# TensorE's period in a decoder's self-attention: the two pairs for the maxima moved behind the fourth score and the small product

## What is computed

```python
q, k, v = proj(Wq, bq), proj(Wk, bk), proj(Wv, bv)        # 16 heads of 16
attn = einsum('bhld,bhrd->bhlr', q, k) * scale            # 1024 x 1024 per head
dist = clip(arange(L)[None, :] - arange(L)[:, None], -64, 8) + 64
rel  = einsum('bhld,lrd->bhlr', q, dist_emb[dist]) * scale
out  = einsum('bhlr,bhrd->bhld', softmax(attn + rel), v)  # then @ Wo.T + bo
```

## Time and profile before

| | |
|---|---|
| median of 3 runs | 1447.9 us (1444.5 to 1449.9) |
| the profiled execution | 1447.09 us, its span 1445.3 us |
| mean granted TensorE clock | 0.953 |
| PE / PEld busy | 1286.4 / 683.0 us |
| DVE / ACT / POOL busy | 1043.6 / 949.5 / 335.6 us |
| DMA | 273.13 MB, 189 GB/s on average |

### The profile page before, as it was taken

One profiled execution on the slowest core, in us unless ns is written; L12 is line 12 of the kernel. 1 busy time (PEld: TensorE's weight loads), 2 busy tenths in 40 slices (PEclk: granted clock), 3 DMA queues, 4 the chain that ended last, 5 costly groups with the idle time before them and its releaser, 6 DMA issues. The chain is left out here.

```text
span 1445.3 us, 24911 instructions
## 1 busy us (share of the span) xinstructions
PE 1286.4 (89%) x8220; PEld 683.0 (47%) x8220; DVE 1043.6 (72%) x2547; ACT 949.5 (66%) x1666; POOL 335.6 (23%) x567
## 2 busy tenths in 40 slices
PE   7787999999999999999999999999997799910597
PEld 4444344344334334334434434436886587710586
DVE  3376778887887887887887887872564457999655
ACT  4434777777777777777777777773775558959600
POOL 4544121211211211212112112004452002320012
PEclk9999999999999999999999999999998899965799
DMA  8999977877878788697697796526321313825032
GB/s 237 308 335 265 241 206 232 222 202 236 224 215 219 217 234 213 200 260 208 193 259 211 197 249 190 188 74 181 103 74 44 131 59 116 314 87 211 4 113 88
DMA packets 263758, 273.13 MB, mean 189 GB/s; under 512 B 66222, under 2 KB 246990, under 8 KB 259534
## 3 DMA queue, kind: packets, MB, share of 16 engines
q1 hardware_dynamic: 261998, 268.39, 63.9%
q10 hardware_dynamic: 1632, 3.15, 0.7%
HBM read 153.69 MB, written 117.00 MB: 187 GB/s over the span
## 5 line engine op out<-in xcount | busy, mean ns | idle before, releaser
L603 ACT ACTIVATE pr<-scoresT 128x512 f32<-128x512 f32 x1024 | 550.5, 600 | 224.2 <-PE scoresT L851 162.9
L847 PE MATMUL scoresT<-qT,kT 99*128 99x512 bf16 (+7 forms) x1408 | 359.2, 326 | 5.5 <-DVE attn_out L740 2.3
L695 DVE CUSTOM_DVE_ANT_0 junk<-scores_for_max,win 128x200 f32<-128x200 f32 (+2 forms) x512 | 180.1, 352 | 172.4 <-PE scores_for_max L822 162.3
L700 DVE TENSOR_REDUCE mx<-scores_for_max 128x1 f32<-128x888 f32 (+6 forms) x448 | 301.6, 673 | 0.0
L698 DVE TENSOR_REDUCE mx<-scores_for_max 128x1 f32<-128x64 f32 (+6 forms) x448 | 277.4, 619 | 0.0
L864 PE MATMUL attn_out<-pr,vS 128*17 128x512 f32 x2048 | 271.1, 601 | 6.0 <-DMA vS<-v_all 5.9
L847 PEld LDWEIGHTS scoresT<-qT,kT 99*128 99x128 bf16 (+1 forms) x1408 | 113.6, 97 | 335.6 <-ACT rows L580 97.8
L851 PE MATMUL scoresT<-idf,win 128*128 128x128 f32 x1024 | 218.2, 274 | 0.0
L477 POOL COPY rows<-rows 128x736 f32<-128x736 f32 x128 | 102.2, 798 | 391.4 <-ACT rows L580 391.4
L821 PE MATMUL scores_for_max<-kX,qT 64*128 64x512 bf16 x512 | 164.8, 384 | 4.3 <-DVE mx L700 3.0
L822 PE MATMUL scores_for_max<-kX,qX 64*128 64x512 bf16 x512 | 164.7, 384 | 0.0
(11 more groups left out here) (203 smaller groups left out, 1757.3 us busy)
## 6 DMA issues: line engine op xcount, KB each, us to landing
rel_table<-rows SPq DMA_DIRECT2D x128, 512.0 KB, 4.8
win<-rel_table SPq DMA_DIRECT2D x128, 512.0 KB, 5.4
up_raw<-xT_normed SPq DMA_DIRECT2D x6, 1536.0 KB, 9.3
xT_normed<-up_raw SPq DMA_DIRECT2D x6, 1536.0 KB, 6.9
qT<-q_parts SPq DMA_DIRECT2D x32, 256.0 KB, 7.4
kX<-k_parts SPq DMA_DIRECT2D x64, 128.0 KB, 4.8
kT<-k_parts SPq DMA_DIRECT2D x32, 256.0 KB, 5.5
q_parts<-shared SPq DMA_DIRECT2D x32, 192.0 KB, 4.6
```

The lines of the kernel that those rows point to most:

```text
L603: nc.scalar.activation(pr[:, n % NPR, h, :], bank, ACT.Exp).then_inc(t_read, 1)
L695: last = nc.vector.tensor_tensor_reduce(junk[:, n % 2, 0:z - a], bank[:, a:z], win[:, T % NW, q4, h, u:u + z - a], 1.0, NEG, ALU.add, ALU. ...
L700: last = nc.vector.tensor_reduce(mx[:, T % 2, q4, h, 2:3], bank[:, z:L], AX.X, ALU.max)
L847: last = mm(bank[:, a:e], k[0:r], q[0:r, a:e], start=(n == 0), stop=not near and n == len(pieces) - 1, skip_group_check=True)
```

## The change

TensorE's fourth score and the small product go ahead of the two pairs. Before: three scores, two pairs, the fourth score, the small product, the weighted sums. Now: four scores, the small product, two pairs, the weighted sums. What each instruction computes, its waits and the other engines' programs are as they were.

```diff
@@ -882,17 +882,16 @@
 
             for T in range(NT):
                 for kt in range(TL):
-                    for h in range(G - 1):
+                    for h in range(G):
                         scores(T, kt, h)
-                    for c in chunks_of(T, kt):
-                        max_chunk(*c)
-                    scores(T, kt, G - 1)
                     if kt in ROW_AT and T + 3 < NT:
                         make_row(T + 3, ROW_AT[kt])
                     if kt == OUT_AT and T:
                         turn_out(T - 1)
                     if kt == SHIFT_AT and T + 1 < NT:
                         turn_shift(T + 1)
+                    for c in chunks_of(T, kt):
+                        max_chunk(*c)
                     if kt:
                         weigh(T, kt - 1)
                     elif T:
```

## The result

The changed kernel takes 1507.4 us (median of 4 runs, 1506.0 to 1508.5) against 1448.1 before: a ratio of 1.0409, with a 95% interval of 1.0389 to 1.0429. It is 59 us slower, where 59 were forecast (1506).

What follows compares the result with a forecast made beforehand. The order of TensorE's instructions in the self-attention loop was taken to set the time. Tiles 2 to 28 add 57.7 us, the edges 3.5, rounding takes off some 2: +59 on 1447.1 gives 1506, range 1474 to 1532.

Steps and rivals of the forecast that it cites:

- s3's wait: Fourth score waits for ScalarE's exp of the first to free its bank: starts 1.08 into kind A, no wait in kind C.
- kind A: Loop period (one key tile) whose scores each hold no 128x128 transposes: a score .22 us, period 2.86 before, 3.41 forecast.
- kind C: Loop period (one key tile) whose scores each hold two 128x128 transposes: a score .45 us, period 3.64 before.
- The product's wait: Small product waits for the exp of the second score: starts 1.66 into kind A, 1.88 into kind C.
- The two steps taken from neighbours: Product to pair .22, pair to weighted sums .32, from the nearest steps; each may be off by 24 us either way.
- One switch less: Each period with pairs has one turn between kinds of TensorE matmul less: -.10 us.
- mcol's chain: Work from kt 3's pairs through VectorE and POOL to mcol: turned shift in even tiles' kt 5 at 2.03, not 1.66.
- only s3 waits: Rival: the product follows the fourth score at once, except in kt 1; 25 us slower, 1472; chance .08.
- the chain also delays the next tile: Rival: the pairs' delay also hits the turned shift or the next tile's start; 27 us more, 1533; chance .12.
- the drain decides: Rival: at the fourth score and product banks are read in time, each period only loses .10; 1423; chance .04.
- the 57.7 of the sum: Growth of tiles 2 to 28 in us: 14 even at +2.35 and 13 odd at +1.91, 32.9 + 24.8.
- The edges: Query tiles 0, 1, 29, 30, with first loads or without row products: estimated to grow by 3.5 us.

Runs made afterwards that it cites:

- the split run: Kernel before, in every period with pairs the second pair moved behind the fourth score, the first left ahead of it: 1474.0 us, 1.0169 of before.

## Why the prediction was right

- **s3's wait** (1.08 in kind A, none in kind C) came out to the hundredth. The rows that carried it were those of the loop's last tiles, where the old program already ran four scores in a row.
- **The product's wait** (1.66 in kind A, 1.88 in C) too; the run with the pairs between s3 and the product shows that it, with the pairs queued behind it, costs more than s3's own wait (35 against 24 us).
- **The two steps taken from neighbours**, product to pair and pair to weighted sums, were put at .22 and .32 and measured .22 and .31. They made most of the range. For the second the nearest row was all there was, and that it held was not assured. The prediction says that neither occurs in the trace before. For the first that is wrong: ahead of the loop, where `make_row` is followed by a max chunk, the same trace shows it, .22, so its 24 us either way could have been left out (kernel before, TensorE's timeline):

```profile
83.39 0.30 PE L795 MATMUL scoresT<-embS,qT 96*128 96x72 bf16 x4
83.61 0.39 PE L821 MATMUL scores_for_max<-kX,qT 64*128 64x512 bf16 x1
```

- **One switch less** is worth .10 as forecast, and where nothing else waits it is gained. The Trainium skill says, without a figure, that changing the tiling mode drains TensorE (TensorEngine Tiling (Array Packing), Key Properties); the .10 saved here and the .20 added by the split run agree. As the forecast of the whole, -24 us, that rule would have had the wrong sign.
- **mcol's chain** in even kt 5: turn at 2.01, forecast 2.03; its weight, 6 us, was shown by moving it. In odd tiles nothing was charged; the turn comes at 1.92 and not at 1.88, .03 to .04 too late by the same chain.
- **The rivals.** That only s3 waits fell with the first timeline. That the chain also delays the next tile did not happen: the last period of a tile and the first of the next last 3.15 and 3.40 (even to odd) and 3.14 and 3.63 (odd to even), with 3.17, 3.41, 3.17 and 3.63 worked out, so no tile begins with a wait. That the drain decides was out by the loop's own rows.
- **Small misses that cancel:** the tiles 2 to 28 grew by 55.7 us together, which is the 57.7 of the sum less the 2 taken off for rounded terms. The edges (T 0, 1, 29, 30) grew by 2.3 us and not 3.5. The 2.6 us outside the loop were not forecast, and are within what two runs of one kernel differ by (1444.5 to 1449.9 before). That the total came within 2 us is in that part luck; the tiles are not.

## What to carry to other kernels

Where results pass through a short ring of PSUM banks, ask of each instruction which ready work stands between the entry it displaces and itself; that work is cover. Moving it elsewhere lays the wait bare, here .42 us for s3 in kind A (1.08 against .66), though the reading engine was busy for only 19.79 of 26.30 us of the loop. What queues behind a waiting instruction decides the price: here the same pairs that had covered one wait stood behind another. Look for a stretch of the same trace in which the new order already occurs; its starts price the change without a run.

## What was not expected

A period that got shorter by itself made the next one longer by four times as much (.10 against .41), through two max banks and an engine that was busy for only 21.25 of 26.30 us. And a second pair that is issued .65 later, at the price of two more switches, made a period .24 shorter (3.28 to 3.04), because at its old place it had waited for VectorE; the waits view had the waits of this kind on record at 36.7 us, but only the split run showed which part of it was to be had.
